# A gated low-rank residual on one core: who rounds and who subtracts in the opening, and in what order the products of the first two tiles run

## The reference, cut to what matters

```python
base   = einsum('btd,od->bto', x, W)                 # 64*32 tokens, D = 512, O = 512
logits = einsum('btd,ed->bte', x, Wr) + 5.0 * one_hot(ids, 8)
topw, topi = top_k(logits, 2)
gates  = one_hot sum of softmax(topw)                # 8 experts, two of them non-zero
h      = einsum('btd,erd->bter', x, A)               # rank 16 for each of 8 experts
lora   = einsum('bter,bte,eor->bto', h, gates, B)
out    = x + base + 2.0 * lora
```

## Time and profile before

| what | value |
|---|---|
| median of 3 runs | 81.17 us (80.80, 81.17, 81.37) |
| profiled execution | 80.93 us, of which span 79.1 us |
| PE busy | 74.6 us (94% of the span), 505 matmuls |
| DVE, ACT, POOL busy | 51.1, 22.6, 22.8 us |
| granted TensorE clock | full speed in every slice |
| chain that ended last | PE 78%, DMA 7%, DVE 6% |

### The profile page before, as it was taken

How to read it: one execution, slowest core, us unless ns; L and a number is a source line. 1 busy time by engine, 2 the same in 40 slices (tenths; PEclk the granted TensorE clock), 3 DMA queues, 4 the chain that set the end, 5 groups by cost and what they waited for, 6 DMA issues and landing times.

```text
span 79.1 us, 1625 instructions
## 1 busy us (share of the span) xinstructions
PE 74.6 (94%) x505; PEld 70.5 (89%) x505; DVE 51.1 (65%) x216; ACT 22.6 (29%) x57; POOL 22.8 (29%) x25
## 2 busy tenths in 40 slices
PE   6996999799999999999999999999999999999960
PEld 2376998799998999999999999999999999999950
DVE  0183898878588828466482928284664979787670
ACT  4329931514221414050231314140503113111200
POOL 4034880063360141506050513315060605000000
PEclk9999999999999999999999999999999999999999
DMA  1999991597399479999810000270000008032124
GB/s 14 305 375 382 428 425 71 90 419 294 50 373 377 56 301 434 402 244 408 345 71 0 0 0 0 99 298 0 0 0 0 0 37 360 0 133 93 39 102 167
DMA packets 3748, 14.23 MB, mean 180 GB/s; under 512 B 416, under 2 KB 1056, under 8 KB 3488
## 3 DMA queue, kind: packets, MB, share of 16 engines
q1 hardware_dynamic: 3600, 13.98, 47.4%
q10 hardware_dynamic: 144, 0.20, 0.8%
HBM read 9.99 MB, written 4.19 MB: 179 GB/s over the span
## 4 chain that ended last, share of the span: by engine, by line
PE 78%; DMA 7%; DVE 6%; SPq 2%; ACT 1%; issue 1%; DVEq 0%
PE heads_ps L402 36%; PE base_ps L402 25%; DMA first_sb<-in_first 7%; PE heads_ps L434 5%; PE base_ps L434 5%; PE ghT_ps L425 2%; PE base_ps L438 2%; PE heads_ps L438 2%; DVE b_lo L359 2%; DVE w_lo L342 1%; SPq L167 1%; ACT w_hi L224 1%; SPq L165 1%; DVE out_sb L328 1%; ACT x_hi L221 1%
## 5 line engine op out<-in xcount | busy, mean ns | idle before, releaser
L205 POOL TENSOR_TENSOR x_lo<-xT_sb,x_hi 128x512 fp32r<-128x512 f32 x14 | 18.5, 1318 | 39.0 <-ACT x_hi L231 39.0
L402 PE MATMUL heads_ps<-w_hi,x_hi 128*128 128x392 f32 x64 | 22.7, 361 | 0.6 <-ACT w_hi L224 0.6
L402 PE MATMUL heads_ps<-w_hi,x_lo 128*128 128x392 f32 x64 | 21.6, 340 | 0.0
L402 PE MATMUL heads_ps<-w_lo,x_hi 128*128 128x392 f32 x64 | 21.5, 340 | 0.0
L402 PE MATMUL base_ps<-w_hi,x_lo 128*128 128x256 f32 x64 | 18.0, 281 | 0.0
L402 PE MATMUL base_ps<-w_hi,x_hi 128*128 128x256 f32 x64 | 17.8, 283 | 0.0
L402 PE MATMUL base_ps<-w_lo,x_hi 128*128 128x256 f32 x64 | 17.8, 280 | 0.0
L402 PEld LDWEIGHTS heads_ps<-w_hi,x_hi 128*128 128x128 f32 x64 | 12.0, 190 | 1.9 <-ACT x_hi L221 1.3
L235 ACT ACTIVATE ghT_hi<-ghT_ps 128x128 fp32r<-128x128 f32 x15 | 4.1, 277 | 30.9 <-PE ghT_ps L425 30.9
L278 DVE TENSOR_TENSOR ghT_lo<-ghT_ps,ghT_hi 128x128 fp32r<-128x128 f32 x15 | 4.4, 290 | 12.7 <-ACT ghT_hi L235 12.6
L402 PEld LDWEIGHTS base_ps<-w_lo,x_hi 128*128 128x128 f32 x64 | 12.1, 189 | 0.0
(11 more groups left out here) (43 smaller groups left out, 92.0 us busy)
## 6 DMA issues: line engine op xcount, KB each, us to landing
x_sb<-in_x SPq DMA_DIRECT2D x4, 768.0 KB, 5.6
out<-out_sb SPq DMA_DIRECT2D x4, 768.0 KB, 3.9
xT_sb<-in_xT SPq DMA_DIRECT2D x3, 768.0 KB, 4.3
first_sb<-in_first SPq DMA_DIRECT2D x3, 454.0 KB, 5.1
xT_sb<-in_xT SPq DMA_DIRECT2D x1, 1024.0 KB, 6.4
x_sb<-in_x SPq DMA_DIRECT2D x1, 1024.0 KB, 9.5
out<-out_sb SPq DMA_DIRECT2D x3, 256.0 KB, 2.0
xT_sb<-in_xT SPq DMA_DIRECT2D x1, 256.0 KB, 6.0
```

Source lines behind the costliest of these rows:

```text
L205: nc.gpsimd.tensor_tensor(x_lo[:, s, :], xT_sb[:, t - len(FIRST), :], x_hi[:, s, :].bitcast(FP32), ALU.subtract).then_inc(x_lo_made, 1)
L402: return nc.tensor.matmul(dst, xs[:, s, chunks[k]], ws[:, k, cols], start=(k == 0 and n == 0), stop=(k == KC - 1 and n == 2))
```

## The change

Four edits.

1. The high heads weights of chunk 1 are rounded by DVE (`heads_upper(1)`, right when the chunk has landed) and no longer by ACT, which keeps the base part. On DVE the same rounding for chunk 0 now stands ahead of `bias`, which moves behind the two low parts of chunk 0.
2. The low weights of chunks 1 to 3 are made in two DVE instructions each (heads, then base) and not in one.
3. `b_lo` is made by POOL, between low x of tile 2 and low x of tile 3, and no longer by DVE. The factor 2 is no longer in `b_hi` and `b_lo`; the denominator of the gates is halved for it, as a second operation of the instruction that was there.
4. PE: in chunks 1 and 2 the two heads products come ahead of the two base products of each kind; the low-weight products wait for heads and base apart. Chunk 3 goes by kinds as well: the first ones need only the high parts, the heads are finished for both tiles before the base products that need low operands. POOL's loop over tiles starts one tile later, with tile 2 ahead of it.

```diff
--- before.py
+++ after.py
@@ -209,10 +209,14 @@
                 pool.wait_ge(chunk_hi_made, k + 1)
                 nc.gpsimd.tensor_tensor(x_lo[:, 0:2, chunks[k]], first_x[k],
                                         x_hi[:, 0:2, chunks[k]].bitcast(FP32), ALU.subtract).then_inc(chunk_lo_made, 1)
+            x_lower(2, 2)
+            pool.wait_ge(b_hi_made, 1)
+            nc.gpsimd.tensor_tensor(b_lo[:, :], b_sb[:, :], b_hi[:, :].bitcast(FP32),
+                                    ALU.subtract).then_inc(b_lo_made, 1)
             with pool.Fori(0, GROUPS) as g:
-                for j in range(2, 2 + SLOTS):
+                for j in range(3, 3 + SLOTS):
                     x_lower(SLOTS * g + j, j % SLOTS)
-            for t in range(2 + GROUPED, TILES):
+            for t in range(3 + GROUPED, TILES):
                 x_lower(t, t % SLOTS)
 
         @block.scalar
@@ -247,11 +251,10 @@
             for k in range(1, KC):
                 act.wait_ge(chunk_landed[k - 1], 16)
                 chunk_upper(k)
-                for cols in ((heads_cols, base_cols) if k == 1 else (all_cols,)):
-                    w_upper(k, cols)
+                w_upper(k, base_cols if k == 1 else all_cols)
             x_upper(2, 2, xT_third, 16)
             act.wait_ge(b_landed, 16)
-            nc.scalar.activation(b_hi[:, :], b_sb[:, :], ACT.Copy, scale=SCALING).then_inc(b_hi_made, 1)
+            nc.scalar.activation(b_hi[:, :], b_sb[:, :], ACT.Copy).then_inc(b_hi_made, 1)
             exponential(0)
 
             def step(t, j, landed, count):
@@ -293,7 +296,7 @@
                 dve.wait_ge(top_at_made, t + 1)
                 nc.vector.tensor_copy(top_atf[:, :], top_at[:, 0:2]).then_inc(top_atf_made, 1)
                 dve.wait_ge(e2_made, t + 1)
-                nc.vector.tensor_scalar(den[:, :], e2[:, :], 1.0, None, ALU.add).then_inc(den_made, 1)
+                nc.vector.tensor_scalar(den[:, :], e2[:, :], 1.0, 1.0 / SCALING, ALU.add, ALU.mult).then_inc(den_made, 1)
 
             def gates(t):
 
@@ -342,22 +345,29 @@
                 nc.vector.tensor_tensor(w_lo[:, k, cols], w_sb[:, k, cols], w_hi[:, k, cols].bitcast(FP32),
                                         ALU.subtract).then_inc(w_lo_made, 1)
 
+            def heads_upper(k):
+                nc.vector.tensor_copy(w_hi[:, k, heads_cols], w_sb[:, k, heads_cols]).then_inc(wh_hi_made, 1)
+
+            dve.wait_ge(wh_landed, 16)
+            heads_upper(0)
+            dve.wait_ge(wh_hi_made, 1)
+            w_lower(0, heads_cols)
+            dve.wait_ge(w_hi_made, 1)
+            w_lower(0, base_cols)
             dve.wait_ge(expert_made, 1)
             dve.wait_ge(x_landed, 16)
             nc.vector.tensor_scalar(bias[:, :], expert[:, :], ids_sb, LANG_BIAS, ALU.is_equal,
                                     ALU.mult).then_inc(bias_made, 1)
-            dve.wait_ge(wh_landed, 16)
-            nc.vector.tensor_copy(w_hi[:, 0, heads_cols], w_sb[:, 0, heads_cols]).then_inc(wh_hi_made, 1)
-            dve.wait_ge(wh_hi_made, 1)
-            w_lower(0, heads_cols)
-            dve.wait_ge(w_hi_made, 1)
-            w_lower(0, base_cols)
-            for k in range(1, KC):
-                dve.wait_ge(w_hi_made, k + 2)
-                w_lower(k, all_cols)
-            dve.wait_ge(b_hi_made, 1)
-            nc.vector.scalar_tensor_tensor(b_lo[:, :], b_sb[:, :], SCALING, b_hi[:, :].bitcast(FP32), ALU.mult,
-                                           ALU.subtract).then_inc(b_lo_made, 1)
+            dve.wait_ge(chunk_landed[0], 16)
+            heads_upper(1)
+            dve.wait_ge(wh_hi_made, 2)
+            w_lower(1, heads_cols)
+            dve.wait_ge(w_hi_made, 2)
+            w_lower(1, base_cols)
+            for k in range(2, KC):
+                dve.wait_ge(w_hi_made, k + 1)
+                w_lower(k, heads_cols)
+                w_lower(k, base_cols)
             best_two(0, 0)
             gates(0)
             gated(0, 0)
@@ -395,15 +405,15 @@
 
         @block.tensor
         def _(pe):
-            def product(dst, s, cols, k, n):
+            def product(dst, s, cols, k, n, last_n=2):
 
                 xs = x_lo if n == 2 else x_hi
                 ws = w_lo if n == 1 else w_hi
                 return nc.tensor.matmul(dst, xs[:, s, chunks[k]], ws[:, k, cols],
-                                        start=(k == 0 and n == 0), stop=(k == KC - 1 and n == 2))
-
-            def heads_product(s, k, n):
-                return product(heads_ps[s][:, 0:HEADS], s, heads_cols, k, n)
+                                        start=(k == 0 and n == 0), stop=(k == KC - 1 and n == last_n))
+
+            def heads_product(s, k, n, last_n=2):
+                return product(heads_ps[s][:, 0:HEADS], s, heads_cols, k, n, last_n)
 
             def base_product(s, k, n):
                 return product(base_ps[s][:, 0:BASE], s, base_cols, k, n)
@@ -484,36 +494,34 @@
             pe.wait_ge(w_lo_made, 2)
             for t in FIRST:
                 base_product(t, 0, 1)
-            for k in range(1, KC - 1):
+            for k in range(1, KC):
                 pe.wait_ge(chunk_hi_made, k + 1)
                 if k == 1:
+                    pe.wait_ge(wh_hi_made, 2)
+                else:
+                    pe.wait_ge(w_hi_made, k + 1)
+                for t in FIRST:
+                    heads_product(t, k, 0)
+                if k == 1:
                     pe.wait_ge(w_hi_made, 2)
-                    for t in FIRST:
-                        heads_product(t, 1, 0)
-                    pe.wait_ge(w_hi_made, 3)
-                    for t in FIRST:
-                        base_product(t, 1, 0)
-                else:
-                    pe.wait_ge(w_hi_made, k + 2)
-                    for t in FIRST:
-                        heads_product(t, k, 0)
-                        base_product(t, k, 0)
+                for t in FIRST:
+                    base_product(t, k, 0)
                 pe.wait_ge(chunk_lo_made, k + 1)
                 for t in FIRST:
-                    heads_product(t, k, 2)
-                    base_product(t, k, 2)
-                pe.wait_ge(w_lo_made, k + 2)
+                    heads_product(t, k, 2, last_n=1)
+                if k < KC - 1:
+                    for t in FIRST:
+                        base_product(t, k, 2)
+                pe.wait_ge(w_lo_made, 2 * k + 1)
                 for t in FIRST:
-                    heads_product(t, k, 1)
+                    last = heads_product(t, k, 1, last_n=1)
+                    if k == KC - 1:
+                        last.then_inc(heads_done, 1)
+                pe.wait_ge(w_lo_made, 2 * k + 2)
+                for t in FIRST:
                     base_product(t, k, 1)
-            pe.wait_ge(chunk_hi_made, KC)
-            pe.wait_ge(w_hi_made, KC + 1)
-            pe.wait_ge(chunk_lo_made, KC)
-            pe.wait_ge(w_lo_made, KC + 1)
-            for t in FIRST:
-                heads(t, (KC - 1,)).then_inc(heads_done, 1)
-            for t in FIRST:
-                base(t, (KC - 1,)).then_inc(base_done, 1)
+                    if k == KC - 1:
+                        base_product(t, k, 2).then_inc(base_done, 1)
 
             tile_ready(2)
             heads(2, (0, 1))
```

## The result

| | before | changed |
|---|---|---|
| median of 20 runs | 81.34 us (80.80 to 81.97) | 80.93 us (80.40 to 81.49) |
| profiled execution | 80.93 us, span 79.1 us | 80.91 us, span 79.1 us |

The ratio is 0.996, 95% interval 0.9941 to 0.998: faster by 0.33 us (0.16 to 0.48), less than 1%. The forecast's sum was 0.57 us, so the direction was right and the size too large. The two profiled executions alone would show no difference at all, and that is the first thing to explain.

The account below looks back on a forecast made before the run. PE, fully busy from 22.6 to 66.2 us, makes the opening worth what it moves the first transpose: 14.45 to 13.88, with other parts at nothing. The 0.57 us gain gives 80.36 or 80.60, stated as 80.5; range 80.1 to 81.3.

Parts of the forecast that it names:

- The forecast's sum: Tile 0's logits from 12.29 to 11.72 us, its transpose from 14.45 to 13.88: 0.57 us gained.
- What bounds the kernel: PE is busy throughout 22.6 to 66.2 us, so an opening edit is worth what it moves the first transpose, 14.45 us.
- the sentence that PE has no hole there which the change touches: Behind the first transpose of `gh` (14.45 us), PE was said to have no hole that this change touches.
- The exclusion of subtractions: Two subtractions from SBUF on DVE and POOL exclude each other; the waiting one goes next, ending 0.29 to 1.14 us after release.
- I take POOL first: In chunk 1, POOL's low x beats DVE's low heads despite their 0.03 us lead; PE ends the chunk 0.34 us earlier.
- rival 2: DVE wins at 6.55 us in chunk 1, so logits start at 12.04: gain 0.25 us, time 80.68; chance 0.13.
- I cost this at nothing: Tile 0's `second` starting inside POOL's `b_lo` was priced at nothing; bounds nothing and 1.07 us.
- rival 1: The cast of tile 0 is held by `b_lo` on POOL: gain 0.29 us, time 80.64; chance 0.2.
- the 5.48 of the forecast: Forecast transpose of tile 0 at 13.88 us, read against ACT's start on chunk 3 at 8.40.

Follow-up runs that it names:

- e9: The changed kernel again, unaltered, against the kernel before: ratio 0.9958 (0.9923 to 0.9993).
- e13: The changed kernel a third time, unaltered, against the kernel before: ratio 0.9953 (0.992 to 0.9986).
- e10: Repeat of e1, the changed kernel with `b_lo` on POOL waiting for the gate of tile 0: ratio to before 0.9973 (0.9946 to 0.9999).
- e5: The changed kernel with DVE's low heads weights of chunk 1 waiting for POOL's low x of chunk 1: ratio to before 0.9974.
- e11: The changed kernel with the added waits of e1 and e5 together: ratio to before 0.9985 (0.9954 to 1.0017).
- e14: Repeat of e11, the changed kernel with the waits of e1 and e5: ratio to before 0.9966 (0.9933 to 0.9999).
- e6: The changed kernel with the waits of e1 and e5, POOL's tile 2 behind DVE's last low weights, chunk 3 heads first: ratio to before 0.9935.
- e15: Repeat of e6, the changed kernel with the same four edits, over six runs: ratio to before 0.9881 (0.9841 to 0.9921).
- e16: The edits of e6 on the changed kernel without the wait of e5, over six runs: ratio to before 0.9896 (0.9849 to 0.9943).
- e3: The kernel before with only `b_lo` moved to POOL and the factor 2 to the denominator: ratio to before 0.9998 (0.9965 to 1.0032).
- e12: The changed kernel with low weights of chunks 2 and 3 in one DVE instruction each: ratio to before 0.9968 (0.9949 to 0.9987).
- e8: The changed kernel with PE's chunk 3 in the order of the kernel before: ratio to before 1.006 (1.0026 to 1.0094).
- e7: The changed kernel with a spare POOL subtraction of the same size right behind `b_lo`: ratio to before 1.0121 (1.0081 to 1.0161).
- e1: The changed kernel with `b_lo` on POOL waiting for the gate of tile 0: ratio to before 0.9961 (0.9923 to 0.9998).
- e2: The changed kernel with `b_lo` back on DVE ahead of the chain of tile 0: ratio to before 1.001 (0.9973 to 1.0047).
- e4: The changed kernel with the high heads weights of chunk 1 back on ACT: ratio to before 0.9969 (0.994 to 0.9998).

## Why the prediction was right in direction and wrong in size

The openings of the kernel before, of the changed one, and of those with a stall taken away, one profiled execution each, in us. "Rest" is the profiled device time less the transpose. The other seven profiles have rests of 66.35 to 66.67:

| kernel | L1 | L3 | logits | cast | transpose | behind L3 | rest |
|---|---|---|---|---|---|---|---|
| before | 6.08 | 8.40 | 12.29 | 0.17 | 14.45 | 6.05 | 66.48 |
| changed | 5.97 | 8.81 | 12.07 | 0.42 | 14.50 | 5.69 | 66.41 |
| changed, e9 | 6.13 | 8.42 | 12.14 | 0.17 | 14.32 | 5.90 | 66.41 |
| changed, e13 | 6.12 | 9.30 | 12.33 | 0.59 | 14.92 | 5.62 | 66.40 |
| `b_lo` behind gate, e10 | 5.95 | 8.73 | 11.96 | 0.17 | 14.13 | 5.40 | 66.42 |
| POOL first, e5 | 6.00 | 8.78 | 12.05 | 0.42 | 14.48 | 5.70 | 66.39 |
| both, e11 | 6.14 | 8.89 | 12.13 | 0.17 | 14.31 | 5.42 | 66.44 |
| both, e14 | 6.43 | 8.78 | 12.70 | 0.17 | 14.88 | 6.10 | 66.39 |
| combined, e6 | 5.71 | 8.69 | 11.54 | 0.17 | 13.72 | 5.03 | 66.37 |
| combined, e15 | 5.54 | 9.38 | 12.18 | 0.17 | 14.36 | 4.98 | 66.37 |
| e16 | 5.32 | 8.46 | 11.40 | 0.17 | 13.58 | 5.12 | 66.38 |

**What bounds the kernel: right but for 0.1 us.** The rest is 66.37 to 66.48 us in every row, so the opening is worth what it moves the first transpose, and nothing behind it gave anything back. But 66.48 is the kernel before: the sentence that PE has no hole there which the change touches left something out. In the kernel before the `second` of tile 3 was held for 1.07 us beside POOL; in the changed kernel it comes 0.37 us earlier, ahead of POOL's subtraction, and isn't. That instruction, and the transpose of tile 4 in both kernels (PE before, DVE and PE changed):

```profile
29.04 0.27 PE L425 MATMUL ghT_ps<-ident,gh 128*128 128x128 f32 x1
...
22.12 0.29 DVE L304 TENSOR_SCALAR second<-expert,top_atf,e 128x8 f32<-128x8 int32 x1
...
28.98 0.27 PE L435 MATMUL ghT_ps<-ident,gh 128*128 128x128 f32 x1
```

The transpose of tile 4 is 14.59 behind that of tile 0 before and 14.48 in the changed kernel (14.49 in e9): 0.1 us between these executions lies here and not in the opening. The held `second` is the likely reason, since e3, the other profile that has one (1.39 us at 23.04), has 14.58 and the highest rest, 66.67; a held `gate` in e12 (1.20 us at 22.95) cost nothing (14.48). No run tested it alone.

**The exclusion of subtractions: right.** The durations worked out from it came within 0.02 us (10.71, 12.14 and 13.28 above), in e8 PE's start at 12.24 too. The order of two near starts is what it couldn't tell.

**Chunk 1, "I take POOL first": failed.** I put DVE's low heads 0.03 ahead of POOL's low x, from a start of the cast a little behind ACT's. The cast starts with ACT (5.97 and 5.97 in the changed kernel), the lead is 0.09 us, and with that DVE wins. This was rival 2, to which I gave 0.13; in e9, the execution with the landings of before, it came as priced: products at 7.74 for 7.75, logits at 12.14 for 12.04, against 11.72 in the forecast.

**`b_lo`, "I cost this at nothing": failed in part of the executions.** I priced the hold of `second` and left the cast out of the sum, since no row showed one beside a POOL subtraction. It is held, for 0.25 us in the first profile of the changed kernel, 0.42 in e13 and 1.09 in e7. This was rival 1 (0.29 for the whole gain). The page that it cites, the Trainium skill's SBUF — State Buffer, "Who interferes with whom", is borne out by that for a cast of two columns. Were the sum made with that rule alone, it would have been 0.29 us; that 0.33 was measured beside it is luck in part, since chunk 1 went wrong as well and 0.1 us came from behind the transpose.

**Which of the two shows depends on the landing.** Where ACT starts on chunk 3 long after chunk 1 (2.84 us in the changed kernel's first profile, 3.18 in e13), `b_lo` still runs when the cast comes. Where it starts soon after (2.29 us in e9, 2.33 in e12), `b_lo` is over or nearly, and logits wait for PE until 6.01 and 5.99 behind L1; in the forecast they came 5.64 behind it. Either costs: 5.62 to 5.90 behind L3, 0.14 to 0.42 more than the 5.48 of the forecast.

**What isn't shown.** That these two stalls are the missing 0.2 us is seen execution by execution, not in medians: with one or both taken away (e1, e5, e10, e11, e14) the ratios are 0.9961 to 0.9985, no better than the 0.9953 to 0.996 of the changed kernel. Each removal helps in one kind of execution, and the one in chunk 1 makes a new wait in the low bases (e14). Of the eighteen profiles, nine have ACT's starts on chunks 1 and 3 between 2.26 and 2.45 us apart, nine between 2.62 and 3.84; how often each kind occurs in unprofiled runs can't be read from them. There is one profile of the kernel before, so what is read against its 6.05 rests on one execution. I also took one execution's landings as the base: the profile of before had the earliest start on chunk 3 of all, and the twenty runs have a median of 81.34, not the 81.17 of three.

**By edits:** neither the move of `b_lo` alone (e3, 0.9998) nor the chunk edits alone (e2, 1.001) show a gain clear of the scatter; together they give 0.996. PE's order in chunk 3 is needed beside the low bases that now end late (e8, 1.006); the cast of chunk 1 on DVE (e4) and the split low weights of chunks 2 and 3 (e12) are not.

## What to carry to other kernels

Where VectorE and GpSimd both read SBUF, put every instruction of both on one line in time, with the one that waits going next, as in the rows here, and look at the smallest instructions of a latency chain first: a two-column cast was held for 1.09 us by a subtraction of 1.28 us. Read a difference of a few tenths of a microsecond against the landing of the loads in the same execution, and take more than one profile before a sum is made on one. Taking away a stall by a wait can move it by one instruction (e14). What gained 1% here was a set of edits that finish the chain's operands first, on PE (tile 0's heads first) and on DVE (POOL's next tile behind the last low weights), with `b_lo` behind the gate.

## What the runs showed of the hardware that I had not expected

- A cast of 128x2 was held by a GpSimd subtraction for 1.09 us (e7, 1.26 against 0.17). Not every DVE instruction is held: logits, the two largest and their places ran at 12.07 to 12.85 in the changed kernel, beside `b_lo`, in 0.17, 0.17 and 0.16 us; the kernel before has 0.15, 0.17 and 0.16.
- A few hundredths of a microsecond decide who is held. In the kernel before the same `gate` took 1.33 us with a lead of 0.02 on POOL and 0.23 with a lead of 0.12 (57.39 against 57.51); `second` was held with leads of 0.04 and 0.07 (e3, 23.04 against 23.11); DVE's low heads of chunk 1 won with 0.09 (6.37 against 6.46). But the lead alone isn't all: DVE's low bases of chunk 2, which follow its low heads at once, won with 0.02 (9.28 against 9.30, and POOL took 0.98 where it takes 0.73 alone). What makes the difference is not shown.
- Landings of the same loads scatter by more than the whole effect: ACT's start on chunk 3 lay between 8.40 and 9.38 us in the table above.
- PE's first two heads products of chunk 0 together took 0.64 us in the kernel before and 0.99 in the changed one, with the same operands; no wait is shown, and the cause stayed open. It isn't the change: e9 and e13, the same kernel, have 0.70 and 0.61.
